# Layer norm statistics taken tile by tile, a wait placed later, and the second batch's steps one tile sooner in a fused four-layer kernel

## The reference

```
x = x + tanh(g_xattn[0]) * L0_xattn(layernorm(x), ctx)     # 16 heads, clipped softmax
x = x + tanh(g_ffn[0])   * L0_ffn(layernorm(x))            # 8 experts, top 2, shared
x = x + tanh(g_xattn[1]) * L1_xattn(layernorm(x), ctx)     # "memory attention", one head of width 256
x = x + tanh(g_ffn[1])   * L1_ffn(layernorm(x))            # 8 experts, top 2, shared
x = x + tanh(g_xattn[2]) * L2_xattn(layernorm(x), ctx)     # 16 heads, queries rounded to int8
x = x + tanh(g_ffn[2])   * L2_ffn(layernorm(x))            # sign weights
x = x + tanh(g_xattn[3]) * L3_xattn(layernorm(x), ctx)     # 16 heads, two key sets
x = x + tanh(g_ffn[3])   * L3_ffn(layernorm(x))            # 16 experts, top 6, shared
```

## Time and profile before

| | |
|---|---|
| median of 3 runs | 1122.41 us (1118.03 to 1123.39) |
| the profiled execution | 1120.06 us, of which the span from first to last instruction is 1118.3 us |
| mean granted TensorE clock | 0.953 of full speed |
| PE busy | 1001.5 us, 90% of the span |
| DVE, ACT, POOL busy | 731.0, 580.6, 408.5 us |
| memory attention | about 317 to 355 us of the span |
| feed-forward of layer 1 | about 355 to 465 us |
| third attention | about 465 to 618 us |

### The profile page before, as it was taken

The page is one execution under the profiler, slowest core; times in us unless marked ns, Lnnn a source line. Parts: engine busy times, 40 slices in busy tenths (PEclk is TensorE's granted clock), DMA queues, the critical chain, the costliest instruction groups (busy, mean ns, idle before and its releaser), DMA issues.

```text
span 1118.3 us, 18120 instructions
## 1 busy us (share of the span) xinstructions
PE 1001.5 (90%) x6456; PEld 760.5 (68%) x6456; DVE 731.0 (65%) x1629; ACT 580.6 (52%) x1129; POOL 408.5 (37%) x521
## 2 busy tenths in 40 slices
PE   3899878998988998789999776799999899999997
PEld 2666546787877887565664575566555588888886
DVE  6467755757867556778888666876676365445444
ACT  3688853454533554236667442265565545554553
POOL 5524403445414445432223035324210144444452
PEclk9899978999998999879999998899999899999999
DMA  7955714465530468945521255734521244556553
GB/s 178 245 109 123 170 36 129 137 169 156 156 108 1 117 175 187 171 85 125 130 54 41 76 128 123 153 91 85 123 48 33 61 138 124 158 139 184 159 154 102
DMA packets 82067, 136.54 MB, mean 122 GB/s; under 512 B 11565, under 2 KB 40518, under 8 KB 79546
## 3 DMA queue, kind: packets, MB, share of 16 engines
q1 hardware_dynamic: 71034, 101.93, 31.4%
q0 software_dynamic: 10944, 33.45, 17.3%
HBM read 113.41 MB, written 22.97 MB: 122 GB/s over the span
## 4 chain that ended last, share of the span: by engine, by line
PE 65%; DVE 16%; ACT 5%; DMA 5%; POOL 4%; issue 4%; SPq 1%; DVEq 0%; ACTq 0%; POOLq 0%
PE psum L621 42%; PE psum L914 7%; PE psum L881 6%; PE psum L890 5%; ACT probs L1063 2%; DMA ff_w<-weights_out 2%; PE psum L840 1%; DVE nmx L1379 1%; DVE nmx L1376 1%; DVE nmx L1377 1%; POOL keys L1126 1%; PE psum L722 1%; DVE probs L1470 1%; POOL ff_wl L1937 1%; DMA keys<-keys_out 1%
## 5 line engine op out<-in xcount | busy, mean ns | idle before, releaser
L621 PE MATMUL psum<-ff_xh,ff_wh 128*128 128x512 f32 x424 | 173.7, 410 | 20.0 <-POOL ff_wl L1937 13.6
L1065 ACT ACTIVATE probs<-psum 128x512 f32<-128x512 f32 x256 | 144.4, 597 | 78.7 <-PE psum L881 75.1
L881 PE MATMUL psum<-queries,keys 128*128 128x512 f32 x384 | 157.8, 441 | 12.9 <-ACT probs L1063 5.8
L1937 POOL TENSOR_TENSOR ff_wl<-ff_raw,ff_wh 128x512 fp32r<-128x512 f32 x92 | 118.8, 1291 | 100.6 <-ACT ff_wh L1889 100.6
L621 PE MATMUL psum<-ff_xh,ff_wl 128*128 128x512 f32 x392 | 155.0, 395 | 0.0
L890 PE MATMUL psum<-keys,queries 128*128 128x512 f32 x256 | 117.9, 477 | 17.0 <-DVE nmx L1377 8.2
L621 PE MATMUL psum<-ff_wh,ff_hh 128*128 128x256 f32 x456 | 128.9, 286 | 4.1 <-DVE ff_hl L1992 3.9
L621 PE MATMUL psum<-ff_wh,ff_hl 128*128 128x256 f32 x456 | 128.5, 286 | 0.0
L1982 DVE TENSOR_TENSOR psum<-ff_s,psum 128x512 f32<-128x512 f32 x98 | 68.2, 696 | 86.8 <-PE psum L621 85.7
L914 PE MATMUL psum<-probs,values 128*32 128x256 f32 x1664 | 112.1, 392 | 2.9 <-DVE probs L1470 2.7
L1942 POOL TENSOR_TENSOR ff_wl<-ff_raw,ff_wh 128x256 fp32r<-128x256 f32 x92 | 69.7, 758 | 122.8 <-ACT ff_wh L1896 122.7
(11 more groups left out here) (271 smaller groups left out, 2194.4 us busy)
## 6 DMA issues: line engine op xcount, KB each, us to landing
ff_w<-weights_out SPq DMA_DIRECT2D x94, 256.0 KB
ff_raw<-in_ff SPq DMA_DIRECT2D x92, 256.0 KB, 4.1
ff_raw<-in_ff SPq DMA_DIRECT2D x106, 128.0 KB, 2.1
keys_out<-keys_turned SPq DMA_DIRECT2D x24, 512.0 KB, 3.7
keys<-keys_out POOLq DMA_DIRECT2D x48, 256.0 KB, 5.1
queries_out<-queries_turned SPq DMA_DIRECT2D x24, 256.0 KB, 4.4
keys<-keys_out POOLq DMA_DIRECT2D x48, 128.0 KB, 5.4
queries<-queries_out POOLq DMA_DIRECT2D x32, 192.0 KB, 3.7
```

Source lines behind the costliest of these rows:

```text
L621: last = eng.matmul(dst, lhs[i](k), rhs[j](k), start=start and n == 0, stop=stop and n == groups * len(pairs) - 1, skip_group_check=True)
L881: then(eng.matmul(dst, kst[buf(c)][:, pair, kt * P:(kt + 1) * P], qst[buf(c)][:, :, pair, :], start=True, stop=True, skip_group_check=True ...
L1065: ins = eng.activation(dst, src, ACT.Exp, scale=SCALE)
L1937: then(eng.tensor_tensor(ff_wl[:, slot, 0:2 * D], raw(n)[:, 0:2 * D], ff_wh[:, slot, 0:2 * D].bitcast(F32), ALU.subtract), "f_w1r")
```

## The change

Three parts. First, in the memory attention DVE takes the bn_stats of each of the first four tiles right behind the add that completes the tile (with a wait for that add), in rounds 2 to 5; `statistics` is called with `taken=True` and only aggregates. Its hook goes from round 6 to 5, `normal` from 7 to 6, `turn` and `halves` from 8 to 7. Second, TensorE's wait for `f_acc` goes from the start of the attention's main part to the first maxima product of batch 0; in the last attention that product is TensorE's first step anyway, so nothing moves there. Third, in `LEADS[2]` the steps of batch 1 stand one tile sooner, and `q` and `kk` of batch 1 join behind n = 18.

```diff
          12: [("ln", 0)], 13: [("lm", 0)], 14: [("kr", 0, 0), ("xt", 0), ("xe", 0)],
-         15: [("kr", 0, 1), ("q", 0), ("kk", 0, 2)],
-         16: [("tq", 0), ("qe", 0), ("qw", 0), ("ln", 1)],
-         17: [("kt", 1, 0), ("ke", 1, 0), ("lm", 1)],
-         18: [("kt", 1, 1), ("ke", 1, 1), ("xt", 1), ("xe", 1)]},
+         15: [("kr", 0, 1), ("q", 0), ("kk", 0, 2), ("ln", 1)],
+         16: [("tq", 0), ("qe", 0), ("qw", 0), ("kt", 1, 0), ("ke", 1, 0), ("lm", 1)],
+         17: [("kt", 1, 1), ("ke", 1, 1), ("xt", 1), ("xe", 1)],
+         18: [("q", 1), ("kk", 1, 2)]},
...
-MEMORY_HOOKS = {5: [("clear",)], 6: [("statistics", 0)], 7: [("normal", 0)], 8: [("turn", 0), ("halves", 0)]}
+MEMORY_HOOKS = {5: [("clear",), ("statistics", 0)], 6: [("normal", 0)], 7: [("turn", 0), ("halves", 0)]}
...
             def maxima(st):
                 _, b, k = st
                 pair, m, qt = k // 4, k // 2 % 2, k % 2
+                if (b, k) == (0, 0):
+
+                    wait(eng, "f_acc", ACC_DONE[blk])
...
-            def begin():
-                if blk:
-                    wait(eng, "f_acc", ACC_DONE[blk])
-
-            return Run(do, begin)
+            return Run(do)
...
                     then(eng.scalar_tensor_tensor(x[:, t, :], psum[:, t % 2, 0:D], small[:, 4 + t % 2:5 + t % 2],
                                                   x[:, t, :], ALU.mult, ALU.add), "c_x")
+                    if t < 4:
+                        wait(eng, "c_x", t + 1)
+                        ins = eng.bn_stats(stat[:, 4 + t, :], x[:, t, :])
+                        if t == 3:
+                            dl(ins)
```

More of the change, by code:

```diff
@@ L1612, in root, with statistics @@
             then(eng.tensor_tensor(rstd[:, 4:8], ve[:, 4:8], half_neg[:, 4:8], ALU.pow), "f_pout")
-        def statistics(self, eng, h):
-            for t in range(4):
-                last = eng.bn_stats(stat[:, 4 + t, :], x[:, 4 * h + t, :])
-            link(eng, "dve", last)
+        def statistics(self, eng, h, taken=False):
+            if not taken:
+                for t in range(4):
+                    last = eng.bn_stats(stat[:, 4 + t, :], x[:, 4 * h + t, :])
+                link(eng, "dve", last)
             for t in range(4):
@@ L2398, in main @@
                     elif name == "statistics":
-                        wait(eng, "c_x", 4)
-                        ff_parts[1].statistics(eng, 0)
+                        ff_parts[1].statistics(eng, 0, taken=True)
                     elif name == "normal":
```

## The result

| kernel | runs | median, us | kernel before beside it | ratio, 95% interval | us against before |
|---|---|---|---|---|---|
| the change | 6 | 1113.99 | 1122.90 | 0.9935 (0.9910 to 0.9959) | -7.3 (-10.1 to -4.6) |
| the change, second series | 12 | 1115.02 | 1121.19 | 0.9948 (0.9922 to 0.9974) | -5.8 (-8.7 to -2.9) |

The change is faster, by 0.65% and 0.52%. The time lies inside the range of the prediction. The profiled execution of the change is its slowest of the six, 1119.48 us (span 1117.7). It reaches the first memory scores at 323.90 against 317.30, 6.6 us late, in front of anything that the change touches.

A forecast was written before the change was run, and what follows sets the result against it. The chain was 65% TensorE and 16% DVE, with TensorE not full in the two touched stretches. +0.9 - 5.0 = -4.1 us gave 1116.0 from the profiled execution, 1118.3 from the median; predicted 1117.5, range 1112.5 to 1123.

The forecast's parts named there:

- Part 1 in the loop: Memory attention rounds: bn_stats 0.46 each, aggregate, variance and normalising moved; last maximum 1.9 us later, at 348.5.
- the prediction's choice: Memory loop: a bn_stats waiting for the add costs 0.11 us more; with free waits the total is 4.5, not 4.1.
- The sum: Whole kernel: +0.9 us for the memory-loop statistics and -5.0 for the hand-over, together -4.1 us.
- Behind the last maximum: End of memory attention: last weighing 5.6 us after the last maximum begins, against 6.6 before; gain 1.0.
- the bound of 2.6: Memory attention: worst cost of the statistics, if TensorE's clock falls once more and adds about 1.7 us to +0.9.
- Part 3: Layer 1 feed-forward: batch 1's steps one tile sooner, `lm` before the router-weight wait; tile 19's up step ends 1.2 us sooner.
- Part 2: Hand-over to the third attention: TensorE starts 4.5 us sooner, DVE's maxima 5.5; 5.0 taken, bounds 3.3 and 5.7.
- Rival (d): Hand-over: queries from HBM land after the adds, maxima wait; gain 3.6, total -2.7 us; within forecast's range, no separate chance.
- Rival (b): Third attention: head start partly lost in slow-clock stretch, about 1.5 us, `kk` lock 1.3 more; total -1.5, 1120.0; chance 0.22.
- signs of being wrong: Hand-over and after: HBM or low-half waits, longer half-clock stretch, or changed distance from first maxima product to end; no sizes.
- Rival (a): Memory loop: rounds have room for the bn_stats, so statistics cost -0.9; total -5.9 us, 1115.7; chance 0.17.
- Rival (c): Memory rounds 3 to 7: last maximum 1.9 later, TensorE's clock drops again, earlier third attention counts little; +1.6, 1123; chance 0.11.

The follow-up runs named there:

- e8: Changed kernel with the bn_stats of tiles 0 to 2 one round later, not waiting for the add in front; one run, 1116.58 us.
- e12: Changed kernel with GpSimd's low half of the last batch's context cut to eight columns, leaving work out; one run, 1116.95 us.
- e6: Changed kernel with seven DVE memsets as a pause between the last down step and the last adds; 1121.25 us, 0.9988 against the kernel before.
- e1: Kernel before with only the memory-loop statistics tile by tile and the hooks one round sooner; 1124.89 us, ratio 1.0030.
- the change again: The unchanged changed kernel, measured and profiled once more beside the follow-ups, against the kernel before; 1115.02 us, ratio 0.9948.
- e2: Kernel before with only the moved wait for the adds and batch 1's steps one tile sooner; 1112.57 us, ratio 0.9913.
- e10: Kernel before with only the statistics and normalising, placed behind the maxima in DVE's wait for ACT, no hand-over change; 1118.28 us, ratio 0.9972.
- e3: Changed kernel with bn_stats, aggregate, variance and normalising behind the maxima, in DVE's wait for the high half; 1107.42 us, 0.9883 against the kernel before.
- e4: Kernel before with only the wait for the adds moved to the first maxima product, leads as they were; 1120.11 us, ratio 0.9972.
- e7: Changed kernel with its four bn_stats kept but the hooks back in rounds 6, 7 and 8; 1115.06 us, 0.9945 against the kernel before.

## Why the prediction came out as it did

**Part 1 in the loop: right in its terms, one left out.** Each bn_stats costs 0.46 as worked out. The Trainium skill, VectorE: DVE Perf Modes, section The DRAIN you can't avoid, found eight copies no slower with a semaphore behind each. For these bn_stats the trace doesn't agree: e8 against the change measures 0.11 for the wait, so the prediction's choice stands. From round 6 to 7 the -0.5 (1.4 in, 1.9 out) came as 4.82 - 5.33 = -0.51. The last maximum was to be 1.9 later and is 29.87 - 27.24 = 2.6 later. The step that failed is that the aggregate and the variance move from round 6 to round 5 at equal price: in round 5 GpSimd splits the context, and 0.5 of the difference is that (e12). The sum asked about this lock for `kk` alone. The Trainium skill, SBUF — State Buffer, section SBUF: two separate sides, describes the ports that the two engines share as an exclusive lock, held for a whole instruction. The trace agrees: both stretched operations ended within 0.1 us of GpSimd's end.

**Behind the last maximum** the sum had 5.6 us to the last weighing instead of 6.6. There are 6.2 (355.78 to 361.97, where the chain of waits has the last weighing and the matmuls behind it). The walk had left out the gate's low half, 0.88 beside GpSimd's weight split, which stands ahead of the last `pt_lo`:

```profile
360.26 1.70 issue
361.97 4.13 PE psum L621 x35
```

So part 1 costs 2.6 - 0.4 = 2.2 at the last weighing, where +0.9 was said, inside the bound of 2.6. A little further on, from the first maximum to the first low half of the feed-forward, four traces without part 1 have 46.2, 46.2, 46.5 and 48.0 us, and seven with it 47.3 to 48.3: about 1.0 more on the mean, the prediction's size again, with TensorE's clock mixed in. To the weighting of tile 16 it is 1.4 more: 120.0, 120.2, 120.5 and 123.5 without, 120.7 to 123.8 with. The six above 122 have a half-clock stretch of 3.4 us among the first tiles, between 377 and 386 us, that the five others lack; five of the six have part 1. Its run says +3.4 (0.6 to 6.2).

**Part 3** was to move the last down step 1.2 sooner; it is 22.57 - 21.29 = 1.3. `lm` starts right behind the keys' split and ends under the landing router weight, as said. **Part 2:** the first maxima product was to come 4.5 sooner; it is 29.30 - 24.70 = 4.6. The first maximum, 5.5 said, 5.7 found. From the last down step 3.4 us with one wait, as said; the queries had landed. Rival (d) falls.

**The sum took 5.0 for the hand-over and the traces compared show 6.4, the runs 9.8.** Two terms were mis-sized. First, of the 4.5 for TensorE and 5.5 for DVE the prediction took a middle of 5.0; the whole 5.7 at the first maximum carried through. Behind it another 0.7 us came (69.10 - 30.98 = 38.1 against 62.68 - 25.29 = 37.4), with less of that stretch at the half clock, 10 us in 25 instead of 18. Rival (b) had the sign the wrong way round: it feared that sooner work falls into a fixed slow stretch, and the stretch shrank. In e6 a longer idle time brought it back, 18 us where the new hand-over's eight traces have 7 to 14, at about 1 us from the first maximum to `kn`. Second, the sum took DVE's wait of 3.72 and TensorE's of 1.74 for what they cost. They are one draw of a landing: 3.7, 4.7, 5.4 and 7.0 on DVE, 1.7, 1.8, 3.8 and 5.0 on TensorE, in the four traces that have the old leads complete, and behind the longer three TensorE also ran 3.4, 6.8 and 6.8 us at the half clock. The mean distance to `kn` is 3.2 longer than the profiled one. So the wait for the router weight was the right place and the wrong size.

One of the prediction's signs of being wrong did show: the distance from the first maxima product to the end isn't that of before, 649.7 us before and 646.4 after. The means are 650.4 for the old hand-over's three traces and 646.6 for the new one's eight. Of these 3.9 us 1.1 is the maximum that starts sooner behind its product and 0.7 the stretch to `kn`; the 2.1 behind `kn` weren't looked into.

**Rival (a)**, room in the loop, falls: e8 and the change show each bn_stats as longer rounds. **Rival (c)**: its first half is there (last maximum 2.6 later), its second isn't. The memory attention ran at the full clock in the first trace of the change, at a mean of 0.96 in the one before; in e1 and in the change again a half-clock stretch falls right behind it. In the 50 us from the first maximum the seven traces with part 1 have 0 to 3.4 us at the half clock, the four without it 3.4 to 10.2, so no extra fall of the clock before the last weighing was found.

**The forecast** of 1117.5 was 3.5 above the median found. The chances gave most to a change within 0.5%; the two series say 0.65% and 0.52% faster, at the border. That the time fell inside the range is in part luck. Two errors of opposite sign met in the sum: part 1 was taken 1.3 (trace) to 2.5 us (run) too cheap, the hand-over 1.4 to 4.8 us too small. With what the runs gave the sum is 3.4 - 9.8 = -6.4.

What stays open: part 1 costs 3.4 in its run (and 2.5 to 3.9, comparing the change's two ratios with e2's), of which the traces show 2.2 at the last weighing, 1.0 in all at the first low half and 1.4 in all at tile 16. The rest isn't placed, and the interval is wide enough that there may be none. That the router weight lands late because the exchange of keys is on its way at the same time was not tested.

## What to carry to other kernels

A wait that ends with a DMA's landing in a crowded stretch has a length that one profile samples once. Before pricing what it removes, look at it in several executions, and move dependent work in front of it: the wait may stay, but nothing hangs on it. Put small operations where their engine waits for another inside a loop, not between a result and the next start, and look at what GpSimd does there: here the same work cost about 3 us in one place (e1, 0.6 to 6.2) and gave about 3 in the other (e10, 0.0 to 6.3).

## What the runs showed of the hardware

- A VectorE operation that waits for its forerunner's result starts 0.11 us later than one that doesn't (0.46 against 0.35 for a bn_stats of 128x256).
- Beside GpSimd operations of 2.4 and 1.3 us, VectorE operations of 0.17 (e12) and 0.18 (e3) took 0.65 and 0.88 in the change, until GpSimd ended. One more bn_stats in front (e8) didn't lengthen that round: 5.35 against 5.33.
- 4.6 us more of idle time in front of the third attention went with a granted clock of 0.64 instead of 0.80 (0.73 in the second trace of the change) over the next 25 us, and with 1.3 us beyond the wait itself; 1.2 us of transposes in a 1.3 us wait changed neither clock nor time.
- Waits of 3.8 and 5.0 us of TensorE for `xn` went with 6.8 us at the half clock (e10, e1), one of 1.7 us with none (before), one of 1.8 us with 3.4 (e4).
- The same weight block took 10.5 (e7) to 15.3 us (the change again) to land in fourteen executions of nearly the same program.
